# Channel mamba with two feed channels on POOL and one skip product; pixel mamba with one pair of feeds on POOL from repeated rows

## What is computed

```
def mamba_fwd(x, in_w, conv_w, conv_b, xproj_w, dt_w, dt_b, A_log, D, out_w):
    xi, z = split(x @ in_w.T, 2)
    xc = silu(causal_conv4(xi) + conv_b)
    dt, Bm, Cm = split(xc @ xproj_w.T, [dt_rank, dt_rank + 16])
    dt = softplus(dt @ dt_w.T + dt_b)
    dA  = exp(dt[..., None] * -exp(A_log))
    dBx = dt[..., None] * Bm[:, :, None, :] * xc[..., None]
    h[t] = dA[t] * h[t-1] + dBx[t]            # 16 states for each channel
    y = sum_over_states(h * C) + xc * D       # "xc * D" is the skip
    return (y * silu(z)) @ out_w.T
xs: all pixels in one sequence of 64 channels        -> mamba (stage "spa")
xe: for each pixel, 8 tokens of 8 channels           -> mamba (stage "spe")
```

## Time and profile before

| | |
|---|---|
| median of three runs | 7600.77 us |
| the profiled execution's own time | 7609.55 us |
| its span | 7607.1 us |
| busy over the span: PE, DVE, ACT, POOL | 87%, 75%, 52%, 46% |
| stage "spa": first DVE feed to last scan | 3525.5 to 5513.1 us |
| stage "spe": first DVE feed to last scan | 5555.6 to 7368.9 us |

### The profile page before, as it was taken

The page is one execution under the profiler, slowest core; times in us unless marked ns, Lnnn a source line. Parts: engine busy times, 40 slices in busy tenths (PEclk is TensorE's granted clock), DMA queues, the critical chain, the costliest instruction groups (busy, mean ns, idle before and its releaser), DMA issues. The chain is left out here.

```text
span 7607.1 us, 120115 instructions
## 1 busy us (share of the span) xinstructions
...
## 2 busy tenths in 40 slices
...
DMA packets 618033, 481.73 MB, mean 63 GB/s; under 512 B 248797, under 2 KB 549123, under 8 KB 609435
## 3 DMA queue, kind: packets, MB, share of 16 engines
...
## 5 line engine op out<-in xcount | busy, mean ns | idle before, releaser
L2556 DVE TENSOR_TENSOR_SCAN spa_hs<-spa_p_d,spa_hs,spa_bx 128x483 f32<-128x483 f32 x1168 | 1476.2, 1404 | 0.0
L2282 POOL TENSOR_TENSOR spa_hc<-spa_hs,spa_cr 128x966 f32<-128x966 f32 x592 | 1224.4, 2068 | 426.8 <-DVE spa_hs L2556 410.5
L2687 POOL TENSOR_TENSOR spe_hc<-spe_hs,spe_cu 128x1024 f32<-128x1024 f32 x520 | 1216.1, 2359 | 274.6 <-DVE spe_hs L2884 274.6
L2884 DVE TENSOR_TENSOR_SCAN spe_hs<-spe_p_d,spe_bx 128x1024 f32<-128x1024 f32 x520 | 1161.0, 2274 | 6.5 <-ACT spe_p_d L2833 5.9
L1065 DVE TENSOR_REDUCE attention_nm<-attention_p_s 128x2 f32<-128x640 f32 x1024 | 789.1, 812 | 259.2 <-PE attention_p_s L922 258.1
L2761 PE MATMUL spe_p_y<-spe_idt,spe_hc 128*128 128x128 f32 x8320 | 973.3, 275 | 0.0
L2761 PEld LDWEIGHTS spe_p_y<-spe_idt,spe_hc 128*128 128x128 f32 x8320 | 951.7, 192 | 0.0
L1023 ACT ACTIVATE attention_pr<-attention_p_t 128x512 f32<-128x512 f32 x1280 | 710.6, 598 | 418.6 <-PE attention_p_t L945 287.5
L2467 ACT ACTIVATE spa_p_d<-spa_p_d,spa_av 128x483 f32<-128x483 f32 x1184 | 705.1, 634 | 409.6 <-PE spa_p_d L2339 407.6
L2833 ACT ACTIVATE spe_p_d<-spe_p_d 128x896 f32<-128x896 f32 x520 | 445.5, 899 | 795.4 <-PE spe_p_d L2746 795.2
L2542 DVE TENSOR_TENSOR spa_bx<-spa_br,spa_p_u 128x952 f32<-128x952 f32 x592 | 780.0, 1318 | 33.5 <-PE spa_p_u L2352 33.4
...
## 6 DMA issues: line engine op xcount, KB each, us to landing
...
attention_rc<-scratch_den SPq DMA_DIRECT2D x128, 256.0 KB
...
spa_xt<-scratch_x SPq DMA_DIRECT2D x148, 121.5 KB, 2.6
...
scratch_xf<-front_out SPq DMA_DIRECT2D x128, 128.0 KB, 2.5
...
attention_xs<-in_x_dram SPq DMA_DIRECT2D x128, 128.0 KB, 4.7
```

The source lines that it names most:

```text
L2282: nc.gpsimd.tensor_tensor(hc[:, k % 8:k % 8 + 2, :], hs[:, k:k + 2, :], cr2[:, s % 2, :].unsqueeze(1).broadcast_to([128, 2, NA]), ALU.mult ...
L2556: nc.vector.tensor_tensor_scan(hs[:, k, v], p_d[k % 4][:, v], bx[:, k, v], 0.0 if start else hs[:, k, NA - 1:NA], ALU.mult, ALU.add).then_ ...
L2687: nc.gpsimd.tensor_tensor(hc[:, k, :, d, :].rearrange("p s d t -> p d s t"), hs[:, k % 2, d, :, :], rows, ALU.mult)\
L2884: nc.vector.tensor_tensor_scan(hs[:, k % 2, d].rearrange("p d s t -> p (d s t)"), p_d[h][:, :], bx[:, k % 2, d].rearrange("p d s t -> p (d ...
```

## The change

In "spa" pair j = 3 (`OWN`) is taken off DVE and off PE's spreading of u. SP copies the eight rows of u that it needs from `du`, repeated 16 times each, into a new tile `uc` (two DMAs of 128 x 483 a chunk, `spread_own`), and POOL multiplies `br` by `uc` into `bx` (`own_feed`, semaphore `bx_pool`). The counts of the other semaphores follow the seven pairs left (`FED`, `ND`).

```diff
+    OWN = 3
+    FED = [j for j in range(NP) if j != OWN]
+    ND = len(FED)
+        uc = st.sb("uc", [128, 2, NA])
+            def spread_own(c, s, r):
+                sp.wait_ge(u_ready, c + 1)
+                for e in range(2):
+                    i = 32 * (2 * (OWN % 2) + e) + 8 * (OWN // 2)
+                    sp.dma_start(uc[:, e, :], du[i:i + 8, s % 2, 1, :].unsqueeze(1).broadcast_to([8, ST, NA])).then_inc(u_in, 16)
-            stream(sp, NC, UA, HEAD, 4, (0, keep_x), (0, next_load), (3, store))
+            stream(sp, NC, UA, HEAD, 4, (0, keep_x), (0, next_load), (1, spread_own), (3, store))
...
-                after(pool, u_spread, (c - 1) * NP)
+                after(pool, u_spread, (c - 1) * ND)
+                after(pool, u_in, (c - 1) * 32)
...
+                after(pool, bx_pool, c)
+            def own_feed(c, s, r):
+                pool.wait_ge(b_copied, c + 1)
+                pool.wait_ge(u_in, 32 * c + 32)
+                after(pool, scanned, (c - 1) * NBL + (2 * OWN + 2))
+                nc.gpsimd.tensor_tensor(kept(bx[:, 2 * OWN:2 * OWN + 2, :]), b_kept(s), kept(uc[:, :, :]), ALU.mult).then_inc(bx_pool, 1)
-            stream(pool, NC, UA, HEAD, 2, (2, weigh(0, 1)), (1, step_sizes), (2, weigh(1, 6)), (0, silu), (2, weigh(6, 8)))
+            stream(pool, NC, UA, HEAD, 2, (2, own_feed), (2, weigh(0, 1)), (1, step_sizes), (2, weigh(1, 6)), (0, silu), (2, weigh(6, 8)))
...
-                   (2, spread_dt(2)), (2, spread_u(3)), (0, project_x),
-                   (2, spread_dt(3)), (2, spread_u(4)), (3, project_out), (0, project_z),
+                   (2, spread_dt(2)), (2, spread_u(4)), (0, project_x),
+                   (2, spread_dt(3)), (3, project_out), (0, project_z),
...
+                            if j == OWN:
+                                dve.wait_ge(bx_pool, c + 1)
+                            else:
+                                dve.wait_ge(bx_ready, c * ND + (FED.index(j) + 1))
```

```diff
+    DV = DE - 2
-        cu = st.sb("cu", [128, NSUB, 2, TD])
+        bcu = st.sb("bcu", [128, NSUB, 3, TD])
+            def feed(k):
+                def run(c, s, r):
+                    pool.wait_ge(cu_copied, NSUB * c + (k + 1))
+                    after(pool, scanned[1], NSUB * c + (k - 1))
+                    d = slice(DV, DE)
+                    nc.gpsimd.tensor_tensor(bx[:, k % 2, d], steps(k, d), rows_for(bcu[:, k, 0, :], d), ALU.mult).then_inc(bx_pool, 1)
...
+            def skip(c, s, r):
+                pe.wait_ge(x_active, c + 1)
+                after(pe, y_ready, c)
+                nc.tensor.matmul(p_y[:, :], dg[:, :], xz[:, s, 0, :], start=True, stop=False)
...
-                    nc.tensor.matmul(p_y[:, px], dg[:, :], xz[:, s, 0, px], start=True, stop=False)
...
-                   (2, dt_a(2, 1)), (1, b_c_u(0)), (0, project_z), (2, total(0)), (2, dt_a(3, 0)),
+                   (2, dt_a(2, 1)), (1, b_c_u(0)), (0, project_z), (2, skip), (2, total(0)), (2, dt_a(3, 0)),
...
+                    after(act, bx_pool, NSUB * c + (k - 3))
-                    nc.scalar.activation(cu[:, k].rearrange("p q n -> p (q n)"), p_bc[k % 2][:, TD:3 * TD], ACT.Copy).then_inc(cu_copied, 1)
+                    nc.scalar.activation(bcu[:, k].rearrange("p q n -> p (q n)"), p_bc[k % 2][:, 0:3 * TD], ACT.Copy).then_inc(cu_copied, 1)
...
-                    nc.vector.tensor_tensor(bx[:, k % 2], steps, rows, ALU.mult).then_inc(bx_ready, 1)
+                    d = slice(0, DV)
+                    nc.vector.tensor_tensor(bx[:, k % 2, d], steps(k, d), rows_for(p_bc[k % 2][:, 0:TD], d), ALU.mult).then_inc(bx_ready, 1)
...
+                    if h == 1:
+                        dve.wait_ge(bx_pool, NSUB * c + (k + 1))
```

More of the change, by code:

```diff
@@ L2184, in spatial_mamba @@
                                 "b_copied", "c_copied"))
-        (sig_step, sig_ready, activated, dt_step, u_ready) = (
-            st.sem(n) for n in ("sig_step", "sig_ready", "activated", "dt_step", "u_ready"))
+        (sig_step, sig_ready, activated, dt_step, u_ready, u_in, bx_pool) = (
+            st.sem(n) for n in ("sig_step", "sig_ready", "activated", "dt_step", "u_ready", "u_in", "bx_pool"))
         (dt_spread, u_spread, decay_ready, bx_ready, scanned, weighted, summed, y_ready, out_done, out_copied) = (
@@ L2202, in jumps, with kept, b_kept @@
             return rows(t)[:, :, KEPT - 1]
+        def kept(t):
+            return t.rearrange("p k (r w) -> p k r w", w=KEPT)[:, :, :, 0:KEPT - 1]
+        def b_kept(s):
+            return rows(br[:, s % 2, :])[:, :, 0:KEPT - 1].unsqueeze(1).broadcast_to([128, 2, RA, KEPT - 1])
         @block.sync
@@ L2346, in run @@
                     pe.wait_ge(u_ready, c + 1)
-                    after(pe, bx_ready, c * NP + j)
+                    after(pe, bx_ready, c * ND + FED.index(j))
                     for e in range(2):
@@ L2451, in copy_b @@
                 act.wait_ge(b_done, c + 1)
-                after(act, bx_ready, NP * (c - 1))
+                after(act, bx_ready, ND * (c - 1))
+                after(act, bx_pool, c - 1)
                 nc.scalar.activation(br[:, s % 2, :], p_x[:, 0:NA], ACT.Copy).then_inc(b_copied, 1)
@@ L2567, in _ @@
             for j in range(NP):
-                order += [(2, feed(j + 1)) if j + 1 < NP else (1, feed(0)), (2, scan(j))]
+                if j + 1 == NP:
+                    order.append((1, feed(0)))
+                elif j + 1 != OWN:
+                    order.append((2, feed(j + 1)))
+                order.append((2, scan(j)))
                 if j == 1:
@@ L2621, in spectral_mamba, with steps, rows_for @@
                                 "dt_done", "soft_step", "soft_ready", "dt_ready", "u_ready"))
-        (bc_done, cu_copied, bx_ready, summed, y_ready, out_done, out_copied) = (
-            st.sem(n) for n in ("bc_done", "cu_copied", "bx_ready", "summed", "y_ready", "out_done", "out_copied"))
+        (bc_done, cu_copied, bx_ready, bx_pool, summed, y_ready, out_done, out_copied) = (
+            st.sem(n) for n in ("bc_done", "cu_copied", "bx_ready", "bx_pool", "summed", "y_ready", "out_done", "out_copied"))
         dta_done, decayed, scanned, weighted = st.sem2("dta_done"), st.sem2("decayed"), st.sem2("scanned"), st.sem2("weighted")
         block = st.block()
+        def steps(k, d):
+            n = d.stop - d.start
+            return bcu[:, k, 2, d.start * TK:d.stop * TK].rearrange("p (d t) -> p d t", t=TK).unsqueeze(2).broadcast_to([128, n, ST, TK])
+        def rows_for(v, d):
+            return v.rearrange("p (s t) -> p s t", t=TK).unsqueeze(1).broadcast_to([128, d.stop - d.start, ST, TK])
         @block.sync
@@ L2689, in weigh @@
                 return run
[L2691 to L2692 removed]
+            def feed(k):
[4 more added lines that the diff above has]
+                    nc.gpsimd.tensor_tensor(bx[:, k % 2, d], steps(k, d), rows_for(bcu[:, k, 0, :], d), ALU.mult).then_inc(bx_pool, 1)
+                return run
+            stream(pool, NC, UE, HEAD, 2, (2, feed(1)), (1, silu_z), (2, weigh(0, 0)), (1, step_sizes), (2, weigh(0, 1)),
+                   (2, feed(2)), (2, weigh(1, 0)), (2, weigh(1, 1)), (2, feed(3)),
+                   (2, weigh(2, 0)), (2, weigh(2, 1)), (0, silu_x), (1, feed(0)), (2, weigh(3, 0)), (2, weigh(3, 1)))
         @block.tensor
```

18 lines of the change are left out of this document (4 added, 14 removed).

## The result

Four runs of each kernel, in turns on one chip: 7528.25 us after the change (7519.82 to 7550.36), 7606.86 before. The ratio is 0.9901, its 95% interval 0.988 to 0.9921. So the change is faster by 75 to 79 us where 134 were forecast, and the time lies 4 us above the range. The profiled execution is the slowest of the four (7550.36 us), so what it shows of losses is rather too much than too little.

What follows compares the result with a forecast made beforehand. DVE was taken to set the pace in both stages, with PE and POOL close in "spe". 78 us from "spa" plus 70 - 14 = 56 from "spe" gave 7600.8 - 134 = 7467 us; 8-in-10 range 7448 to 7524.

Steps and rivals of the forecast that it cites:

- "spa", one feed less: 78 us: In "spa", DVE drops one feed of eight, 1.05 us in each of 74 chunks: 78 us gained.
- POOL's product, its place, the waits of PE and POOL in "spa": In "spa", POOL's new product takes 2.2 us within its idle time, with no wait for DMAs and nothing due on PE.
- "spe", 70 us less for DVE: In "spe", DVE's feeds shrink by 256 elements, 0.27 us four times a chunk over 65 chunks: 70 us at most.
- "spe", PE gives back 14 us: In "spe", PE comes late behind the 512-column skip, so DVE waits 0.21 us once a chunk: 14 us lost.
- The first: Rival: in "spe" PE or POOL becomes the bound; gain 78 + 0 to 25 us, 7498 to 7523 us; chance 20%.
- The second: Rival: "spa" gives its gain back through PE's separated spreads or POOL's later step sizes; 7545 us; chance 8%.
- The third: Rival: in "spa" the DMAs' rows of u reach POOL's feed late, making it slower; 7771 us; chance 3%.
- The fourth: Rival: DVE and POOL exclude one another, so POOL's new work stops DVE in both stages; 7798 us; chance 2%.
- The sum: Both stages' gains together: 78 us in "spa" and 56 in "spe", 134 us in all.

Runs made afterwards that it cites:

- after_pad30: The changed kernel with 30 idle instructions (waits long satisfied) more in DVE's program ahead of the "spa" loop; ratio to the kernel before 0.9853, "spa" 1906.6 us.

## Why the prediction was right or wrong

- *"spa", one feed less: 78 us.* Right in size. In after_pad30 the stage gains 1983.2 - 1906.6 = 76.6 us. In after itself 42.8 of them are lost again. The step that failed is the cost of the two DMAs, taken as nothing because "the DMA engines are nearly idle here": I took 5 us to landing and asked only who waits for their data, and I had their size wrong: 242 KB is one of them, not both together. They fill 13 us of each chunk, at 49%, and who suffers reads no data of theirs: DVE's own code, whose fetch at the turn then holds DVE's sequencer for 3.3 to 4.8 us. The sum had no term for code at all, and no view that I read showed one, since in the kernel before q14 has one packet there.
- *POOL's product, its place, the waits of PE and POOL in "spa".* Right: 2.13 us, one wait for the DMA (6.8 us, at the start), and in the padded kernel no wait of DVE from 3700 to 5350 us.
- *"spe", 70 us less for DVE.* Right: feeds from start to start of 1.94 us (6503.32 to 6505.26), POOL's products 0.73 us, POOL not the bound.
- *"spe", PE gives back 14 us.* Mis-sized: 70 - 32.4 = 38 us, 0.58 us a chunk in place of 0.21. I took the part of 6.57 us as typical of all four and the skip's part as the only long one, though the one ahead of it, with project_out, took 7.32 us in the kernel before (6499.71 to 6507.03). The part with project_out takes longer than DVE's 6.53, so PE has no slack to make up what the skip costs, and by start times DVE waits 0.43 us in one part (6512.80 - 6510.43 - 1.94) and 0.15 in the next (6519.49). The wait of the skip for the gate was not in the sum either. A chunk is 27.32 us (1776.0 / 65), not 27.0.
- *The rivals.* The first, the pixel stage short of its gain, was half right: 32 us where it gave 0 to 25, and PE was the reason. The second gave 7545 for a DVE that loses its gain in "spa" again; some of that happened, but by another mechanism than either of its two. The third had its eye on the right DMAs, with a loss through the wrong reader. The fourth is excluded: in after_pad30 POOL's product took 2.13 us beside a DVE that never paused, and "spa" kept its gain.
- *The sum.* 33.8 + 32.4 = 66 us in the profiled executions against 134. Of the 68 missing, 43 are the fetched loop, 24 PE in "spe". By the medians 55 to 59 us are missing, since the profiled execution of after is its slowest.
